# Mamba norm: GpSimd adds the four groups of squares, and one sum per chunk is turned into columns

## The reference, cut to what matters

```
zxbcdt = u @ in_w.T                                     # z, xBC, dt
xBC = silu(causal_conv4(xBC) + b)                       # x, B, C
h = h * dA_t + (dt_t * x_t) * B_t ;  y_t = h . C_t      # scan over L = 64
y = (y + x * D) * silu(z)                               # [tokens, 512]
y = y * rsqrt(mean(y*y, axis=-1) + 1e-05) * norm_w
out = y @ out_w.T
```

## Time and profile before

| | |
|---|---|
| median of 3 runs | 2421.56 us (2416.81 to 2422.51) |
| profiled execution, device time | 2419.65 us |
| its span | 2417.9 us |
| mean granted clock of PE | 0.974 of full speed |
| Mamba block, from its first instructions | 1438 us to the end of the span |
| busy share of the span | PE 86%, DVE 85%, ACT 54%, POOL 51% |

### The profile page before, as it was taken

How to read it: one execution, slowest core, us unless ns; L and a number is a source line. 1 busy time by engine, 2 the same in 40 slices (tenths; PEclk the granted TensorE clock), 3 DMA queues, 4 the chain that set the end, 5 groups by cost and what they waited for, 6 DMA issues and landing times. The chain is left out here.

```text
span 2417.9 us, 44041 instructions
## 1 busy us (share of the span) xinstructions
PE 2080.3 (86%) x17272; PEld 1408.8 (58%) x17272; DVE 2059.5 (85%) x2424; ACT 1296.7 (54%) x2834; POOL 1238.8 (51%) x645
## 2 busy tenths in 40 slices
PE   8988977787796676666999978989998999999997
PEld 7867522232242221115788856777777888888886
DVE  4426799999999999995888858999998999999996
ACT  3336677767867774541332335555555555555552
POOL 1102699989999999991110001334333344433434
PEclk9999999999999999998999989999999999999999
DMA  7769312222221213201332224233222234333332
GB/s 235 248 205 251 112 37 54 46 59 54 50 55 20 37 30 65 59 12 30 114 99 79 79 72 75 72 68 80 67 69 71 75 87 98 88 98 101 93 80 62
DMA packets 301359, 204.55 MB, mean 85 GB/s; under 512 B 202080, under 2 KB 279392, under 8 KB 297056
## 3 DMA queue, kind: packets, MB, share of 16 engines
q1 hardware_dynamic: 283120, 147.29, 25.2%
q0 software_dynamic: 8704, 33.56, 3.8%
q10 hardware_dynamic: 9328, 20.88, 3.2%
HBM read 133.76 MB, written 67.90 MB: 83 GB/s over the span
## 5 line engine op out<-in xcount | busy, mean ns | idle before, releaser
L306 DVE TENSOR_TENSOR att_av<-att_att,att_v2ps 128x2816 f32<-128x2816 f32 (+2 forms) x288 | 774.9, 2750 | 20.0 <-PE att_bank L485 17.2
L306 POOL TENSOR_TENSOR att_av<-att_att,att_v2sb 128x1280 f32<-128x1280 f32 x256 | 745.0, 2937 | 36.5 <-PE att_bank L485 32.2
L485 PE MATMUL att_bank<-att_av,att_w 128*32 128x512 f32 x4096 | 535.7, 606 | 220.4 <-DVE att_av L306 201.2
L485 PEld LDWEIGHTS att_bank<-att_av,att_w 128*32 128x32 f32 x4096 | 134.8, 109 | 561.0 <-issue 285.0
L654 ACT ACTIVATE att_ev<-att_bank 128x512 f32<-128x512 f32 x512 | 297.6, 595 | 254.0 <-PE att_bank L485 206.8
L1772 DVE SCALAR_TENSOR_TENSOR mb_cv<-mb_bank,mb_cw,mb_cv 128x504 f32<-128x504 f32 (+2 forms) x480 | 349.4, 733 | 75.1 <-ACT mb_cv L1590 64.6
L1459 PE MATMUL mb_bank<-mb_xT_hi,dt_win_hi 128*128 128x512 f32 x576 | 241.9, 420 | 38.0 <-DVE mb_ms L1816 24.4
L1388 POOL CAST mb_y_hi<-mb_y 128x1024 fp32r<-128x1024 f32 x64 | 67.4, 1054 | 370.1 <-DVE mb_y L1812 370.1
L1393 POOL TENSOR_TENSOR mb_y_lo<-mb_y,mb_y_hi 128x1024 fp32r<-128x1024 f32 x64 | 154.5, 2436 | 181.1 <-DVE mb_S L1781 181.1
L1459 PE MATMUL mb_bank<-mb_xT_lo,dt_win_hi 128*128 128x512 f32 x576 | 232.5, 404 | 0.0
L1459 PE MATMUL mb_bank<-mb_xT_hi,dt_win_lo 128*128 128x512 f32 x576 | 232.0, 403 | 0.0
(11 more groups left out here) (196 smaller groups left out, 3910.3 us busy)
## 6 DMA issues: line engine op xcount, KB each, us to landing
att_xin<-in_x SPq DMA_DIRECT2D x32, 512.0 KB, 4.4
qk_t<-att_qk POOLq DMA_DIRECT2D x16, 1024.0 KB, 5.1
v<-att_vs POOLq DMA_DIRECT2D x16, 1024.0 KB, 5.1
mb_dAb<-dA_rows SPq DMA_DIRECT2D x32, 512.0 KB, 6.3
mb_dAb<-dA_cols SPq DMA_DIRECT2D x32, 512.0 KB, 5.7
mixed_t<-att_ev SPq DMA_DIRECT2D x1020, 8.0 KB
att_q<-qk_t ACTq DMA_DIRECT2D x32, 256.0 KB, 4.7
att_kb<-qk_t ACTq DMA_DIRECT2D x64, 128.0 KB, 3.1
```

Of the source, the lines that this page charges most:

```text
L306: return eng.tensor_tensor(av[t % 2][:, :, d0:d1, :], a.unsqueeze(2).broadcast_to((P, 2, d1 - d0, N)), v2.unsqueeze(1).broadcast_to((P, 2, ...
L485: mm = pe.matmul(bank[r % NB][s * M:(s + 1) * M, :], w[i // WB % 2][:, i % WB, s, :], av[r // 2 % 2][:, i % 2, s * STRIP_D:(s + 1) * STRIP ...
```

## The change

The matmuls of ones over the squares, the four strips, their copy by ACT and the picking vector are gone. POOL adds the squares of groups 0 and 1 to those of groups 2 and 3 (128x1024), waits for itself, and adds the two halves (128x512). PE turns that one sum into four columns with a vector of ones, into bank `G_`. These columns run one loop later than before, behind projection group 4. `project_lo` moves from behind group 3 to behind group 6. On DVE `mean_square` moves from the head of the loop to behind tap group 2, and the four `scale_out` from behind tap group 2 to behind tap group 3. Group 1 no longer waits for `col_read`; the products of B and C do.

```diff
@@ gpsimd
-            pool.memset(pick[:, :], 0.0).then_inc(const_set, 1)
-            pool.wait_ge(const_set, NCONST - 6)
-            for m in range(CT):
-                pool.memset(pick[m * 32:m * 32 + 1, :], 1.0).then_inc(const_set, 1)
+            def add_squares(c):
+                pool.wait_ge(squared, 2 * c + 2)
+                need(pool, col_done, c)
+                pool.tensor_tensor(sq[:, :, :], zs[c % 2][:, 0:2, :], zs[c % 2][:, 2:4, :], ALU.add).then_inc(sq_halved, 1)
+                pool.wait_ge(sq_halved, c + 1)
+                pool.tensor_tensor(sq[:, 0, :], sq[:, 0, :], sq[:, 1, :], ALU.add).then_inc(sq_added, 1)
...
                 if k + 1 < ALL:
                     pool.wait_ge(scanned, PAIR * (k + 2))
+                add_squares(k)
                 y_lo(k, 0)
                 y_lo(k, 1)
                 root(k)
@@ tensor
-                elif m == 0:
-                    need(pe, col_read, c - 1)
-                elif m < CT:
+                elif 0 < m < CT:
                     pe.wait_ge(conv_done, GR * c + m)
@@ products_of_b_c
                 need(pe, s_ready, PAIR * c)
+                need(pe, col_read, c - 1)
@@
-            def sum_squares(c):
-                pe.wait_ge(squared, 2 * c + 2)
-                pe.wait_ge(xtok_copied, PAIR * min(c + 2, ALL))
-                for m in range(CT):
-                    mm = pe.matmul(PR_[1][m * 32:(m + 1) * 32, :], ones[:, :], zs[c % 2][:, m, :], start=True, stop=True)
-                mm.then_inc(ss_done, 1)
-
             def columns(c):
-                pe.wait_ge(ss_copied, c + 1)
+                pe.wait_ge(sq_added, c + 1)
+                pe.wait_ge(s_ready, PAIR * min(c + 2, ALL))
                 for t in range(TT):
-                    mm = pe.matmul(PR_[1][:, t:t + 1], ssr[:, t * P:(t + 1) * P], pick[:, :], start=True, stop=True)
+                    mm = pe.matmul(G_[:, t:t + 1], sq[:, 0, t * P:(t + 1) * P], ones[:, :], start=True, stop=True)
                 mm.then_inc(col_done, 1)
@@ order of loop k on tensor
                     for i in range(NG):
                         group(k + 1, i)
-                        if i == 3 and k > 0:
+                        if i == 4 and k > 0:
+                            columns(k - 1)
+                        if i == 6 and k > 0:
                             project_lo(k - 1)
                 if k == ALL - 1:
+                    columns(k - 1)
                     project_lo(k - 1)
...
                 if k >= 0:
-                    project_hi(k, 0, range(TT))
-                    project_hi(k, 1, range(TT // 2))
-                    sum_squares(k)
-                    project_hi(k, 1, range(TT // 2, TT))
-                    columns(k)
+                    project_hi(k, 0)
+                    project_hi(k, 1)
+            columns(ALL - 1)
             project_lo(ALL - 1)
@@ scalar
-            def copy_sums(c):
-                act.wait_ge(ss_done, c + 1)
-                need(act, col_done, c)
-                act.activation(ssr[:, :], PR_[1][:, :], ACT.Copy).then_inc(ss_copied, 1)
@@ order of loop k on vector
-                if k >= 1:
-                    mean_square(k - 1)
...
                 taps((2, 1), (2, 2), (2, 3))
+                if k >= 1:
+                    mean_square(k - 1)
+                taps((3, 1), (3, 2), (3, 3))
                 for t in range(TT):
                     spare(scale_out, t)
-                taps((3, 1), (3, 2), (3, 3), (4, 1), (4, 2), (4, 3))
+                taps((4, 1), (4, 2), (4, 3))
```

More of the change, by code:

```diff
@@ L1193, in block_mamba @@
         diag = sb("diag", [P, L])
-        ones, pick = sb("ones", [P, 32]), sb("pick", [P, 1])
+        ones = sb("ones", [P, 1])
         neghalf = sb("neghalf", [P, TT])
@@ L1214, in block_mamba @@
         y = sb("y", [P, CT, CHUNK])
-        ssr = sb("ssr", [P, CHUNK])
+        sq = sb("sq", [P, CT // 2, CHUNK])
         ms, rstd = sb("ms", [P, TT]), sb("rstd", [P, TT])
@@ L1242, in block_mamba @@
         wf_hi_ready, y_hi_ready, y_lo_ready = sem("wf_hi_ready"), sem("y_hi_ready"), sem("y_lo_ready")
-        ss_done, ss_copied, col_done, col_read, rstd_ready = (sem("ss_done"), sem("ss_copied"), sem("col_done"),
-                                                              sem("col_read"), sem("rstd_ready"))
+        sq_halved, sq_added, col_done, col_read, rstd_ready = (sem("sq_halved"), sem("sq_added"), sem("col_done"),
+                                                               sem("col_read"), sem("rstd_ready"))
         out_done, out_read = sem("out_done"), sem("out_read")
-        NCONST = 11
+        NCONST = 6
         PARTS = [(0, HN, NT, -1), (1, 0, NT, 6)]
@@ L1509, in y_products, with project_hi @@
                         mm.then_inc(y_done, 1)
-            def project_hi(c, half, tiles):
+            def project_hi(c, half):
                 pe.wait_ge(y_hi_ready, 2 * c + half + 1)
-                for t in tiles:
+                for t in range(TT):
                     if half == 0 and t % 2 == 0:
@@ L1593, in silu_z @@
             def silu_z(c, m):
-                need(act, ss_done, c - 1)
+                need(act, sq_halved, c - 1)
                 if c == 1:
@@ L1685, in _ @@
                     square(k, 1)
-                    copy_sums(k)
                 for n, (_, _, _, first) in enumerate(PARTS):
@@ L1815, in mean_square @@
                 dve.wait_ge(col_done, c + 1)
-                dve.tensor_scalar(ms[:, :], PR_[1][:, 0:TT], 1.0 / DI, EPS, ALU.mult, ALU.add).then_inc(col_read, 1)
+                dve.tensor_scalar(ms[:, :], G_[:, 0:TT], 1.0 / DI, EPS, ALU.mult, ALU.add).then_inc(col_read, 1)
             def scale_out(c, t):
```

## The result

The changed kernel takes 2436.16 us (median of 5 runs, 2433.06 to 2440.35) against 2419.80 us (5 runs) on the same chip: ratio 1.0065, 95% interval 1.0049 to 1.0081. It is slower, by 16 us. The forecast was 2433 us, with a range of 2425 to 2446. The profiled execution took 2440.35 us (span 2438.6, mean granted clock 0.967 against 0.974). It entered the Mamba block 5.5 us later than the profiled execution before; the change touches nothing there, and over the 13 kernels of this document that moment lies anywhere between 1440.0 and 1448.4 us. The other 15.2 us lie in the Mamba block.

A forecast was written before the change was run, and what follows sets the result against it. The bound was taken as a ring of DVE and PE waiting for each other, with POOL's `y_lo` in it. Ring 2.5, step loops 1.3 + 1.3 and tail 8.2 gave +13.3 us on 2419.65: 2433 us, range 2425 to 2446.

The forecast's parts named there:

- The ring: Steady loop: DVE and PE wait for each other, through POOL's `y_lo`; +0.1 us per loop, +2.5 us over 25 loops.
- T: Moment in each loop when the last scan lets DVE go on; the forecast timed its steps from there.
- 0.86 us at the head: Start of the loop: taps start 0.86 us earlier, given back before tap group 4 by columns, two groups and a wait.
- decision point: Before `project_lo`: `y_lo` was covered with 0.8 us; lateness would decide from T + 9.4.
- The end: Last two loops, where nothing covers POOL's adds: +3.6 and +4.6 us, +8.2 in all (6.6 to 8.8).
- The loops with step sizes: Five loops behind step-size work: +0.26 us each, +1.3 in all, plus +1.3 for instructions beside POOL in two.
- contention term: Step-size instructions of DVE in two loops wait for POOL's adds or `y_lo`: +0.65 us each, +1.3 in all.
- same slow stretch: PE in the five step-size loops: matmuls at 0.42 us behind the gap, taken as equal before and after.
- C: Rival: the clock falls in PE's new 1.5 us gap before group 3; +34 us, 2467 us; 6%.
- A: Rival: PE is the bound and gets its work back; faster, 2412 us; 6%.
- B: Rival: the steady loop's gain equals the tail's cost, no change; 2424 us; 17%.
- D: Rival: `y_lo` is late and `project_lo` waits 0.7 us in each loop; +17 us, 2450 us; 7%.

The follow-up runs named there:

- two order experiments: Changed kernel with columns behind projection group 5 in place of 4: 2424.65 us; kernel before, old arithmetic kept, given only the changed order: 2428.65 us.
- third add: Changed kernel with one more 128x512 add on POOL, result unused, between the adds and `y_lo`: 2452.0 us, ratio 1.0133.
- kernels without adds: Changed kernel with columns from one group's squares, no POOL adds: 2430.62 us; kernel before, old arithmetic kept, in the changed order: 2428.65 us.
- two experiments with PE's work: Changed kernel with ten more unused matmuls behind group 2: 2431.06 us; changed kernel with half of `project_hi` left out: 2447.43 us.
- run without adds: Changed kernel without POOL's two adds, columns made from the squares of one of four groups alone: 2430.62 us, ratio 1.0045.
- run with less work: Changed kernel with half of `project_hi` left out (16 of 32 matmuls, low part of the weights): 2447.43 us, ratio 1.0118.
- second try: Kernel before with only `project_lo` moved, from behind group 3 to behind group 4: 2417.46 us, ratio 0.9989.
- third try: Kernel before with `project_lo` behind group 4, mean square on ACT, columns behind group 0 of the next loop: 2411.46 us, ratio 0.9970.

## Why the prediction was right

**The ring.** Measured from T, against the steps of the sum: group 3 at +2.30 (forecast 2.33), columns +5.64 (5.58), group 5 +6.53 (6.50), `project_lo` +9.36 (9.39), tap group 4 +13.56 (13.58; before 13.49). The loop grew by 0.04 us where 0.1 was taken: +0.7 us over the steady loops. That the 0.86 us at the head are given back is shown by the two order experiments.

**POOL.** Adds of 2.36 and 1.30 us (3.6 taken for both), `y_lo` ends at +8.63 (8.6). The third add shows the decision point. The new wait of `silu_z` for the first add was missing from the text. It is up to 2.5 us long. Tap group 2, the first to need a seed behind it, still starts without idle time, but ACT's list has only 0.2 us to spare there (the seed ends at 2179.36 and the taps start at 2179.54).

**The end.** +7.8 us against +8.2. The kernels without adds (59.7 and 59.8 us) show that all of it is theirs.

**The loops with step sizes.** Mis-sized: +3.9 us (0.71 to 0.89 in each of the five) against 1.3 + 1.3. With T at the end of the work on step sizes (where `mean_square` starts before and the first tap after), DVE's timelines split each loop in two, and PE's count the matmuls that come every 0.42 us:

```
loop                                     2      4      7      9     11
from the split to T, after - before   +0.0   +1.0   +0.0   +0.0   +0.9
from T to tap group 4, difference     +0.8   -0.1   +0.8   +0.7   -0.1
slow matmuls, before / after          8/11  11/10   7/10   7/10    9/7
```

The first row is the contention term, and it came as forecast. In loop 4 the third and fourth instruction read, before and then after:

```profile
1600.03 2.44 DVE L1746 SCALAR_TENSOR_TENSOR dt_dt<-dt_dt_x,dt_dt_lnu 128x256 f32<-128x256 f32 x1
```

```profile
1606.09 1.37 DVE L1739 SCALAR_TENSOR_TENSOR dt_dt<-dt_dt_x,dt_dt_lnu 128x256 f32<-128x256 f32 x1
1607.49 2.44 DVE L1742 TENSOR_TENSOR dt_dt_u<-dt_dt,dt_nega 128x256 f32<-128x256 f32 x1
```

The third is 1.1 us shorter, since it waits for the short add, and the fourth 2.0 longer than its 0.42 of the earlier trace rows, since it waits for a `y_lo`. That is +1.9 us in loops 4 and 11 together, where 1.3 was taken. The experiments bear it out. In the kernels without adds T stands 12.6 to 12.7 and 13.7 us behind the split in these loops, and in those with the two adds in the changed place 13.6 and 14.6 to 14.7. With the third add the fourth instruction waits for another short add (1.37 us) in place of a `y_lo`, and T stands at 12.5 and 13.6.

The second row holds the step that failed. The sum said "the same slow stretch". It was not the same: in loops 2, 7 and 9 three more matmuls ran slowly, each 0.19 us longer, which with the 0.26 of the sum makes about the 0.8 of each. In loops 4 and 11 one and two fewer ran slowly, and there the 0.26 is gone. In loop 7, PE's timelines before and after:

```profile
1693.61 0.80 PE L1459 MATMUL mb_bank<-mb_xT_hi,dt_win_hi 128*128 128x512 f32 x1 [3.44 <-DVE mb_ms L1816]
```

```profile
1704.45 0.79 PE L1461 MATMUL mb_bank<-mb_xT_hi,dt_win_hi 128*128 128x512 f32 x1 [4.88 <-DVE mb_cv L1765]
```

The gap grew from 3.44 to 4.88 us. But gaps grew in all five loops, and the number of slow matmuls did not grow in all. It also differs between kernels with the same gap (7 to 10 behind 9.30 us in loop 11), so this part of the difference is to some extent chance.

**Loops 5 and 12.** The term that the sum lacks: +3.4 us. I had used C's price only for the steady loop and its 1.5 us. The two memsets before the taps, a row of the trace before, would have made the gap 2.3 and 2.8 us, inside the span between 1.99 and 2.81 that C left open or at its end. The slow stretch cost 1.1 us in each, since both loops are that much shorter where the clock held (29.55 and 30.53 us). The other 0.6 in each stands with the clock held too: 0.3 from T to tap group 4, as in the sum for loops behind other work, and 0.3 before the next split, where DVE now waits longer for the input that PE transposes.

**Loop 10.** It gained 0.5 us because it had been longer before. DVE's timeline before:

```profile
1785.05 2.92 DVE L1772 SCALAR_TENSOR_TENSOR mb_cv<-mb_bank,mb_cw,mb_cv 128x504 f32<-128x504 f32 x4 [1.70 <-ACT mb_cv L1590]
```

The first seed came 1.70 us late there, in place of the usual 0.72, and after the change this wait is gone. Why the seed was so late in this loop was not followed.

In all 15.2 us on the block against 13.3: the end too large by 0.4, the ring by 1.8, the steps too small by 1.3, loops 5 and 12 not there (3.4), and loop 10 (-0.5). Terms that were too large and terms that were too small nearly cancel, and where an execution enters the block differs by more than the 3 us by which the median missed, so that the number came so close is in part luck. The verdict stood on the ring and the end, and both were right. Against A stand the two experiments with PE's work, against B the end; C did not happen in the steady loops, but in loops 5 and 12 it did, and in three of the loops with step sizes the slow stretch that was there before grew; D stayed 0.7 us away.

## What to carry to other kernels

A wait removed at the head of a loop is worth what the next wait on the same ring leaves of it, so write down the start of each step from one fixed moment, before and after; here that gave each step of the steady loop to 0.1 us. Work moved to an idle engine is free only where something else covers it: price the last rounds of the loop, which have no cover, by themselves. And where a change gathers PE's idle time in one place, look for the rounds in which that gap is longest, for there the clock is likely to fall, and give the price as a range.

## What the runs showed of the hardware

- The granted clock in the kernel after held behind PE's gap of 1.53 us in every steady loop, and fell to 0.50 behind 2.32 and 2.85 us. The length of the gap alone doesn't decide. Behind 2.34 us it held in loop 5 of the run without adds. Behind 2.58 us it held in nine loops and fell in eight of the run with less work. Behind 2.81 us it fell in the kernel before and held in the same loop of the second try. Behind 1.48 us it fell in loop 3 of the third try. The Trainium skill ("TensorE: Matmul & The Clock Gate", Part 1) says that the gate watches on a rhythm of its own, not tied to the kernel, so that the number of slow matmuls differs between runs; these loops agree with it.
- Less work for PE can cost time: 16 matmuls fewer per chunk, 11 us more (run with half of `project_hi`).
- POOL's adds beside DVE's scans: 1.22 us became 2.79 and 1.67, and the adds 2.36 and 1.30 became 3.31 and 2.09. A step-size instruction of 0.42 us took 2.44 beside `y_lo`. Beside taps with one operand in PSUM nothing is seen to be lost (2.90 for four beside the adds, 2.92 beside `y_lo`).
- Eight passes of 128x1 in fp32 take 0.81 us at the full clock; 32 take 3.63, and 6.94 when PE comes out of a gap of 3.61 us.
